# Ten of 28 field pairs of every second tile are stored by three narrower DMAs

## The reference

```
pi, pj = PAIRS[:, 0], PAIRS[:, 1]          # 496 pairs (i, j), i < j
proj = einsum('bpd,pod->bpo', x[:, pi, :], W)
out  = proj * x[:, pj, :]                  # (2048, 496, 64)
```

## Time and profile before

| | us |
|---|---|
| median of 3 runs | 691.28 |
| the profiled execution | 692.27 |
| its span | 690.5 |
| PE busy, share of the span | 597.8 (87%) |
| DVE | 415.0 (60%) |
| POOL | 390.7 (57%) |
| ACT | 205.4 (30%) |
| q1's packets, share of 16 engines | 93.3% |
| q10's packets | 5.8% |

### The profile page before, as it was taken

How to read it: one execution, slowest core, us unless ns; L and a number is a source line. 1 busy time by engine, 2 the same in 40 slices (tenths; PEclk the granted TensorE clock), 3 DMA queues, 4 the chain that set the end, 5 groups by cost and what they waited for, 6 DMA issues and landing times.

```text
span 690.5 us, 8403 instructions
## 1 busy us (share of the span) xinstructions
PE 597.8 (87%) x2704; PEld 372.9 (54%) x2704; DVE 415.0 (60%) x528; ACT 205.4 (30%) x257; POOL 390.7 (57%) x228
## 2 busy tenths in 40 slices
PE   6889979799797989979799797988979799797972
PEld 4556646466464555646466464645646466464641
DVE  0656646576574756647576474856747576474851
ACT  2322414233241332414223241322414224141320
POOL 0745738457474655738557374755738557374651
PEclk9998989899897998989989898997989989898995
DMA  8999999999999999999999999999999999999897
GB/s 332 386 430 425 431 427 429 426 428 427 423 427 429 392 417 411 427 426 407 428 407 431 406 427 428 412 425 376 424 423 405 428 415 423 414 423 427 357 422 316
DMA packets 29754, 285.15 MB, mean 413 GB/s; under 512 B 3312, under 2 KB 3440, under 8 KB 7216
## 3 DMA queue, kind: packets, MB, share of 16 engines
q1 hardware_dynamic: 27584, 270.28, 93.3%
q10 hardware_dynamic: 2160, 14.75, 5.8%
HBM read 24.97 MB, written 260.05 MB: 413 GB/s over the span
## 4 chain that ended last, share of the span: by engine, by line
DMA 37%; POOL 26%; issue 22%; PE 10%; ACT 2%; DVE 1%; POOLq 0%; SPq 0%; DVEq 0%; ACTq 0%
DMA out_dram<-staged 36%; POOL staged L213 26%; PE proj L284 9%; ACT staged L250 2%; DVE staged L326 1%; DMA ident_sb<-ident_dram 1%; PE proj L301 1%; POOLq L212 0%; PE proj L262 0%; ACT x_t L228 0%; SPq L183 0%; POOLq L121 0%; ACTq L249 0%; DVEq L126 0%; SPq L182 0%
## 5 line engine op out<-in xcount | busy, mean ns | idle before, releaser
L284 PE MATMUL proj<-w_sb,x_t 64*128 64x512 f32 (+7 forms) x2432 | 562.3, 564 | 72.5 <-DVE staged L326 70.1
L326 DVE TENSOR_TENSOR staged<-proj,x_sb 128x1024 f32<-128x1024 f32 (+7 forms) x528 | 415.0, 828 | 264.5 <-PE proj L284 187.0
L213 POOL TENSOR_TENSOR staged<-staged,x_sb 128x1024 f32<-128x1024 f32 (+4 forms) x224 | 390.5, 1755 | 284.6 <-ACT staged L250 283.8
L284 PEld LDWEIGHTS proj<-w_sb,x_t 64*128 64x128 f32 x2432 | 339.2, 205 | 288.5 <-issue 132.1
L250 ACT ACTIVATE staged<-proj 128x1024 f32<-128x1024 f32 (+4 forms) x224 | 172.8, 787 | 453.0 <-PE proj L284 344.6
L262 PEld LDWEIGHTS proj<-ident_sb,x_sb 128*128 128x128 f32 x256 | 30.4, 150 | 10.2 <-issue 7.6
L262 PE MATMUL proj<-ident_sb,x_sb 128*128 128x128 f32 x256 | 34.1, 290 | 1.9 <-DMA x_sb<-x_dram 1.9
L228 ACT ACTIVATE x_t<-proj 128x1024 f32<-128x1024 f32 x32 | 31.2, 1022 | 13.7 <-PE proj L262 12.2
L301 PE MATMUL proj<-ident_sb 128*128 128x128 f32 x16 | 3.7, 425 | 5.7 <-DMA ident_sb<-ident_dram 5.7
L301 PEld LDWEIGHTS proj<-ident_sb 128*128 128x128 f32 x16 | 3.3, 227 | 5.7 <-DMA ident_sb<-ident_dram 5.7
L228 ACT ACT_TABLE_LOAD x1 | 1.3, 1283 | 1.2 <-PEq L356 1.2
## 6 DMA issues: line engine op xcount, KB each, us to landing
out_dram<-staged SPq DMA_DIRECT2D x16, 1952.0 KB, 11.4
out_dram<-staged SPq DMA_DIRECT2D x16, 1824.0 KB, 14.2
out_dram<-staged SPq DMA_DIRECT2D x16, 1728.0 KB, 17.3
out_dram<-staged SPq DMA_DIRECT2D x16, 1696.0 KB, 14.8
out_dram<-staged SPq DMA_DIRECT2D x16, 1568.0 KB, 14.3
out_dram<-staged SPq DMA_DIRECT2D x16, 1440.0 KB, 15.7
out_dram<-staged SPq DMA_DIRECT2D x16, 1312.0 KB, 15.6
out_dram<-staged SPq DMA_DIRECT2D x16, 1216.0 KB, 13.8
```

Source lines behind the costliest of these rows:

```text
L213: last = nc.gpsimd.tensor_tensor(product, product, x_sb[tile.parity][:, j * dim:(j + n) * dim], ALU.mult)
L284: last = nc.tensor.matmul(proj[b][h][:, at:at + width], x_t[tile.parity][half, i // 2, :], w_sb[half, col:col + width], start=True, stop=True)
L326: last = nc.vector.tensor_tensor(staged_part(item, i, j, n), proj[b][h][:, at:at + n * dim], x_sb[tile.parity][:, j * dim:(j + n) * dim], ...
```

## The change

In odd tiles the store of group 10 is cut. Its first 18 pairs are stored by one DMA of 128 rows as before. Its last ten pairs (2560 bytes of a row) are stored by three DMAs, of rows 0 to 118, 119 to 125, and 126 and 127. The three use 7, 7 and 2 DMA engines, so that an engine has 17, 1 and 1 rows of them. Each of the three adds 16 to the slot's semaphore too, so the waits for slot 5 count three more DMAs for each pair of tiles. Even tiles, all other groups and the computation stay as they are.

```diff
--- before.py
+++ after.py
@@ -15,6 +15,11 @@
 WARM_UP = 16
 
 SHARED_SLOTS = {9: 4, 10: 5}
+
+
+SPLIT_GROUP = 10
+SPLIT_PAIRS = 10
+SPLIT_ROWS = (119, 7, 2)
 
 
 def pair_index(i, j, fields):
@@ -158,7 +163,10 @@
             k = slot_of[g]
             before = [h for h in range(g) if slot_of[h] == k]
             if not (tile.first and not before):
-                eng.wait_ge(stored[k], tile.number * 16 * slot_uses[k] + 16 * len(before))
+
+                more = len(SPLIT_ROWS) * (slot_of[SPLIT_GROUP] == k)
+                eng.wait_ge(stored[k], tile.half * 16 * (2 * slot_uses[k] + more)
+                            + 16 * (tile.parity * slot_uses[k] + len(before)))
 
         def staged_part(s, i, j, n):
             g = group_of[s]
@@ -180,8 +188,17 @@
                     sp.wait_ge(emptied[b][group[-1] not in pool_steps], use + 1)
                     if pooled and g > 0:
                         sp.wait_ge(pool_scaled[g], tile.number + 1)
-                    sp.dma_start(out[bass.ds(tile.number * P, P), first * dim:(first + n) * dim],
-                                 staged[slot_of[g]][:, 0:n * dim]).then_inc(stored[slot_of[g]], 16)
+                    whole = n - SPLIT_PAIRS if g == SPLIT_GROUP and tile.parity else n
+                    sp.dma_start(out[bass.ds(tile.number * P, P), first * dim:(first + whole) * dim],
+                                 staged[slot_of[g]][:, 0:whole * dim]).then_inc(stored[slot_of[g]], 16)
+                    if whole < n:
+                        row = 0
+                        for rows in SPLIT_ROWS:
+                            sp.dma_start(
+                                out[bass.ds(tile.number * P + row, rows), (first + whole) * dim:(first + n) * dim],
+                                staged[slot_of[g]][row:row + rows, whole * dim:n * dim]
+                            ).then_inc(stored[slot_of[g]], 16)
+                            row += rows
 
             half = fields * dim // 2
             sp.dma_start(x_sb[0][:, 0:half], x[0:P, 0:half]).then_inc(x_first_loaded[0], 16)
@@ -198,7 +215,8 @@
 
             each_tile(sp, emit)
             for k in range(slots):
-                sp.wait_ge(stored[k], 16 * slot_uses[k] * tiles)
+                more = len(SPLIT_ROWS) * (slot_of[SPLIT_GROUP] == k)
+                sp.wait_ge(stored[k], 16 * slot_uses[k] * tiles + 8 * more * tiles)
 
         @block.gpsimd
         def _(pool):
```

## The result

The changed kernel takes 702.38 us, the median of 4 runs (701.73 to 702.57), against 691.34 before. The ratio is 1.0157, with a 95% interval from 1.0146 to 1.0169, which is +10.9 us (+10.1 to +11.7). The time lies in the range (691 to 716) and the direction is as forecast. The forecast was 707, or +15.4 us; about two thirds of that came, and, as the experiments show, mostly by the way of rival (d) and not by the forecast's.

What follows compares the result with a forecast made beforehand. One late DMA engine was taken to bound the run; the first two engines' +23.5 us over eight odd tiles, less 8.1 us of room, gave +15.4 us on 692.3, said as 707 us, range 691 to 716.

Steps and rivals of the forecast that it cites:

- rival (d): Laggard is one of the first seven engines, without room: +8 to +9 us unshared, +22 to +24 shared; chance 0.06.
- One engine bounds the run: Whole run: one late DMA engine of sixteen, about 3.4 us behind at the end, sets the release of staging slots.
- tail of about seven engines: End of the run: a sign of the forecast, about seven engines (share 0.44) or two (0.125) busy after the others.
- The late engine is one of the nine relieved: Odd-tile stores: the laggard is among nine engines without rows of the ten pairs, relieved by 6.3 us over eight tiles.
- rival (b): Whole run gets faster: laggard loses 6.3 us, the seven have more room than the mean; 685 to 690 us; chance 0.12.
- room of 8.1 us: Whole run: additional work any engine but the laggard can take before it bounds; holes 4.7 plus tail 3.4 us.
- A row costs 2 x, 196 ns, because of sharing: 119-row store in odd tiles: shared rows cost twice 98 ns, +23.5 us on the first two engines over eight tiles.
- 1 x: Ten pairs' store: a row of 2560 bytes read without sharing costs one engine 98 ns; then +0.5 us in all.
- the doubled rows: Odd tiles, first two engines: 19 rows each at 196 ns instead of 98, over eight tiles.
- Partial sharing: Rival (c), 119-row store: only part of the rows is slowed, +3 to +9 us, 695 to 701 us; chance 0.16.
- SP's three DMAs at 0.33 us each: After an odd tile's last store: three more issues, 1.0 us per odd tile, beside other work, adding nothing.
- The fifteen others have room: Whole run: the fifteen engines other than the laggard end near 686.0 us and carry 8.1 us less work.

Runs made afterwards that it cites:

- the run on five engines: Changed kernel, but only the last three pairs of odd tiles are split, by DMAs of 125 and 3 rows; 696.16 us, ratio 1.0064.
- pair of four and five engines: Changed kernel with three pairs split by DMAs of 124 and 4 rows (690.21 us, ratio 0.9983) or 125 and 3 (696.16 us, 1.0064).
- ten pairs on half of the rows: Changed kernel, but the ten pairs go out by DMAs of 64, 32 and 32 rows, each over sixteen engines; 694.00 us, ratio 1.0036.
- the cut alone: Changed kernel, but the last ten pairs of odd tiles are stored by one DMA of all 128 rows; 692.39 us, ratio 1.0021.
- miss with two tiles: Changed kernel, but only first (15 pairs) and last tile (10) split, DMAs of 124 and 4 rows, last weight load of 128 rows; 692.10 us, ratio 1.001.
- seven-DMA run: Changed kernel, but the ten pairs go out by DMAs of 96, 7, 7, 6, 5, 4 and 3 rows; 695.16 us, ratio 1.0051.

## Why the prediction was right, and where it was not

The direction was right and the time lies in the range, but that is in part luck: the engine that the sum relieved was in fact loaded, and the price per row was too high.

**One engine bounds the run.** Right. The tail of one engine (0.06) stands at the end of the kernel before, of the changed one and of the run on five engines. The tail of about seven engines that I had named as the sign of the forecast did come (shares of 0.50 and 0.37 from 694 to 696 us), as seven engines with 17 rows each give it; but it doesn't set the end, since one engine goes on alone for about 2.5 us. The pair of four and five engines shows that the time follows what this one engine has to do.

**The late engine is one of the nine relieved.** This step failed. The forecast took it as the condition of its sum, as did rival (b); only rival (d) said otherwise and had a chance of 0.06. By the runs it is the fifth, with 18 rows in the changed kernel. It had no room of 8.1 us: every row counted from the first. By the forecast's own prices the unshared sum of (d) is 8 x 0.98 = +7.8 us, where mine was +0.5. What had spoken for the nine, two engines that are usually slow, goes with DMAs that are issued in another way (see "Which engine is late").

**A row costs 2 x, 196 ns, because of sharing.** Failed in size. The ten pairs on half of the rows cost +1.0 us over the cut, not +6. Reading the 205 GB/s as sharing was right for loads (416 when it was gone), and long rows of a store show it too, with 252 GB/s at full share. For the 119-row store it is there in part: in the changed kernel's last store the share is 0.50 with 139 GB/s, 0.50 x 16 = 8 engines at 17.4 GB/s each for the 26.2 of the earlier trace rows. The other eight are idle by then, so the slowing is among those still at work, most of them on the cut's rows, and doesn't need the owners of the rows. Over the whole run a mean engine's packets take 92.8% of 700.5 us, 650.1 us, some 6 us more than before for the same bytes. And the packet records of the kept traces give the price: a row of 2560 bytes took 0.146 us in the mean of all 1024, 0.119 in the cut alone and 0.140 on halves, where the median is 0.102 in each. So most rows cost 1 x and a few much more, and the mean is 0.03 us above that of the cut alone, not 0.1. The Trainium skill's rule of the 16 ports ("SBUF — State Buffer", "Door 1: The DMA port swizzle") thus holds for the load, while the price that I drew from it for the store was too high: what the rule gives for a steady stream I took for every row.

**Two errors of opposite sign.** Too much room (8.1 us for none) made the sum too small, and the doubled rows (19 x 0.098 x 8 = 14.9 us) made it too large; together they put 6.8 us too much into it. The row that the first two engines have beyond the fifth's adds 0.8, and the cut and an open rest, 3.1 us together, were not in it: that makes the 4.5 us by which the forecast was too high. The measured sum is: ten more rows on the fifth engine, 7.8 us; the cut, 1.5 us by its own run; 1.6 us are left of the 10.9. Partial sharing is the likely owner of the rest, but no run takes it out alone, and the interval of the cut (0.8 to 2.2) is nearly as wide. The end of the changed kernel shows such a loss, and a doubt with it:

```profile
696.84:697.57 0.73, 0.00 (x0) 0.00 (x0) 0.00 (x0) 0.00 (x0) 0.00 (x0) 0.50 0.06 6
696.93:697.57 0.64, 0.00 (x0) 0.00 (x0) 0.00 (x0) 0.00 (x0) 0.00 (x0) 0.50 0.00 0
```

A window counts the packets that start in it. The first holds one row of the late engine (4608 bytes, of the 18 pairs' store) and the last completion of the others: 0.73 us at 6 GB/s, where such a row takes 0.18 us at 26. In this tile alone this costs over 0.5 us. But from 696.93 us on nothing else is under way. If sharing is the reason, it acts with a delay, and no run shows that. The rest stays open.

**SP's three DMAs at 0.33 us each.** The duration was wrong: 1.04 us median, up to 1.97. That they are hidden was not tested by itself; in the one tile shown here the three are done at 357.6 us, 2.7 us before the next store is issued.

```profile
353.63 3.96 SPq L197 DMA_DIRECT2D out_dram<-staged  x3
360.29 0.35 SPq L192 DMA_DIRECT2D out_dram<-staged  x1
```

**The fifteen others have room.** Right, and bounded by the holes: 24 more rows of 768 bytes on four engines in each odd tile still left the kernel faster, 24 more of 2560 in the last tile did not. That fifteen engines end together near 686.0 us was read too roughly: the last of them ends near 686.7.

## What to carry to other kernels

When the DMA share is near one, ask at the end of the span how many engines are still at work: a share of 0.06 is one engine, and its packets and completions tell which. Before moving rows between engines, find out with one such run which engine is the late one; moving work onto it costs in full, and moving it off gains only while the others have room, which, as the miss with two tiles suggests, is only what they have left since they last ran dry. And keep loads and stores at all 128 rows where no reason speaks for less: 64 rows halved the rate of the load, and with twice the bytes the kernel was no slower (-0.7 us, -1.4 to 0).

## What was not expected of the hardware

The late engine was the fifth on both chips on which the end of a run tells it (the seven-DMA run, and the pair on four and five engines); the changed kernel's end only says third to seventh. The DMAs that SP issued right behind the store of the 18 pairs took 1.04 us at the median, where a store issued alone takes 0.33 and the loads issued one behind the other at the start 0.56. Stores over half of the rows or fewer lose less than the load over half did: 252 GB/s against 205, and for rows of 2560 bytes +1.0 us in the whole run.
